# Strassen weight sums on GpSimd in operations of 256 columns, and a reordered pair of tiles

## The reference

```python
def _anemll_linear(x, w, su, sv):
    w_eff = w * (su @ sv)
    return jnp.einsum('bsh,oh->bso', x, w_eff)
a = _anemll_linear(x, gate_w, gate_su, gate_sv)
b = _anemll_linear(x, up_w, up_su, up_sv)
d = jax.nn.silu(a) * b
return _anemll_linear(d, down_w, down_su, down_sv)
...
x = x + _L0_ffn_ref(_L0_cond_ref(x, ...), ...)
x = x + _L1_ffn_ref(_L1_cond_ref(x, ...), ...)
```

## Time and profile before

| | us |
|---|---|
| median of 3 runs (lowest, highest) | 638.68 (638.6, 638.7) |
| the profiled execution's own time | 639.42 |
| its span, first to last instruction | 637.8 |
| PE busy | 627.4 |
| DVE busy | 456.0 |
| ACT busy | 319.6 |
| POOL busy | 244.9 |
| granted TensorE clock, mean | 0.998 of full speed |

### The profile page before, as it was taken

One profiled execution on the slowest core, in us unless ns is written; L12 is line 12 of the kernel. 1 busy time (PEld: TensorE's weight loads), 2 busy tenths in 40 slices (PEclk: granted clock), 3 DMA queues, 4 the chain that ended last, 5 costly groups with the idle time before them and its releaser, 6 DMA issues.

```text
span 637.8 us, 7904 instructions
## 1 busy us (share of the span) xinstructions
PE 627.4 (98%) x2864; PEld 508.0 (80%) x2864; DVE 456.0 (71%) x551; ACT 319.6 (50%) x426; POOL 244.9 (38%) x193
## 2 busy tenths in 40 slices
PE   8999999999999999999999999999999999999996
PEld 6888888888878876778777787878887888788885
DVE  4576654434467998885337888645688998999987
ACT  4685725244635344442113444425557887478860
POOL 2670020000000006752023666440003888959986
PEclk9999999999999999999999999999999999999999
DMA  8650032101021111311012000252123112222203
GB/s 249 158 162 34 26 98 74 66 1 45 20 73 47 54 34 57 142 58 59 34 33 100 33 34 30 66 107 65 56 89 100 62 59 63 99 67 67 82 0 133
DMA packets 24473, 45.18 MB, mean 71 GB/s; under 512 B 9972, under 2 KB 12020, under 8 KB 24372
## 3 DMA queue, kind: packets, MB, share of 16 engines
q1 hardware_dynamic: 21972, 40.80, 20.6%
q0 software_dynamic: 2176, 3.36, 2.0%
q10 hardware_dynamic: 288, 0.52, 0.2%
HBM read 40.74 MB, written 2.10 MB: 67 GB/s over the span
## 4 chain that ended last, share of the span: by engine, by line
PE 86%; DVE 5%; ACT 3%; issue 2%; POOL 1%; DMA 1%; DVEq 0%; SPq 0%
PE ps_down L1830 7%; PE ps_down L1831 7%; PE ps_down L1832 7%; PE ps_up L1830 4%; PE ps_up L1831 4%; PE ps_up L1832 4%; PE ps_m L2008 3%; PE ps_gate L1830 3%; PE ps_gate L1831 3%; PE ps_gate L1832 3%; PE ps_m L2009 3%; PE ps_up L2008 3%; PE ps_gate L2008 3%; PE ps_down L2008 3%; PE ps_up L2009 3%; PE ps_gate L2009 3%
## 5 line engine op out<-in xcount | busy, mean ns | idle before, releaser
L805 POOL TENSOR_TENSOR act_lo<-up,act_hi 128x512 fp32r<-128x512 f32 x14 | 18.2, 1297 | 199.0 <-ACT act_hi L1076 199.0
L1830 PE MATMUL ps_down<-act_hi,w_hi 128*128 128x512 f32 (+1 forms) x180 | 71.0, 394 | 0.0
L1831 PE MATMUL ps_down<-act_lo,w_hi 128*128 128x512 f32 (+1 forms) x180 | 70.3, 391 | 0.0
L1832 PE MATMUL ps_down<-act_hi,w_lo 128*128 128x512 f32 (+1 forms) x180 | 70.1, 389 | 0.0
L836 POOL TENSOR_TENSOR up_sum<-up_sum,up_more 128x1024 f32<-128x1024 f32 x14 | 33.8, 2411 | 66.3 <-DVE up_more L1400 66.3
L1285 DVE TENSOR_TENSOR w_lo<-w_raw,w_hi 128x512 fp32r<-128x512 f32 (+4 forms) x41 | 44.4, 1083 | 15.2 <-ACT w_hi L907 10.0
L907 ACT ACTIVATE w_hi<-w_raw 128x1024 fp32r<-128x1024 f32 (+4 forms) x30 | 27.0, 900 | 44.3 <-DVE w_raw L1292 22.3
L1830 PEld LDWEIGHTS ps_down<-act_hi,w_hi 128*128 128x128 f32 (+1 forms) x180 | 33.8, 188 | 7.4
L1832 PEld LDWEIGHTS ps_down<-act_hi,w_lo 128*128 128x128 f32 (+1 forms) x180 | 33.8, 188 | 7.2
L1831 PEld LDWEIGHTS ps_down<-act_lo,w_hi 128*128 128x128 f32 (+1 forms) x180 | 33.8, 188 | 6.7
L1400 DVE SCALAR_TENSOR_TENSOR gate_sum<-ps_up,s_group,gate_sum 128x1024 f32<-128x1024 f32 x28 | 35.8, 1280 | 4.3 <-PE ps_up L2009 4.2
(11 more groups left out here) (297 smaller groups left out, 1845.1 us busy)
## 6 DMA issues: line engine op xcount, KB each, us to landing
w_int<-in_ffn_gu SPq DMA_DIRECT2D x14, 512.0 KB, 3.5
w_raw<-in_cond_gu SPq DMA_DIRECT2D x9, 512.0 KB, 4.0
w_raw<-in_ffn_gu SPq DMA_DIRECT2D x9, 512.0 KB, 3.4
w_raw<-in_ffn_dn SPq DMA_DIRECT2D x8, 448.0 KB, 3.3
w_int<-in_ffn_dn SPq DMA_DIRECT2D x8, 448.0 KB, 3.2
xp<-in_x SPq DMA_DIRECT2D x8, 256.0 KB, 5.6
w_raw_third<-in_ffn_gu SPq DMA_DIRECT2D x4, 512.0 KB, 3.5
xp<-in_x SPq DMA_DIRECT2D x1, 2048.0 KB, 9.9
```

What stands on the lines that cost most here:

```text
L1830: nc.tensor.matmul(ps[0:m, :], w_hi[0:r, s, cols], rhs_hi(k, r), start=start and n == 0, stop=False)
L1831: nc.tensor.matmul(ps[0:m, :], w_hi[0:r, s, cols], rhs_lo(k, r), start=False, stop=False)
L1832: last = nc.tensor.matmul(ps[0:m, :], w_lo[0:r, s, cols], rhs_hi(k, r), start=False, stop=stop and n == len(ks) - 1)
```

## The change

GpSimd's block sums and low parts of 512 columns are split into two instructions of 256 columns each; the signal to the other engines stands on the second one. Ahead of a pair of tiles, GpSimd makes the next tile's sums ahead of both low parts of the former tile. ScalarE copies product 2 of a tile (tile 2's: even ahead of the Silu that ends tile 1) before it writes either high part of the former tile. VectorE scales part 0 of the next pair ahead of the former tile's two products. PE's and SP's queues are unchanged.

```diff
--- before.py
+++ after.py
@@ -792,18 +792,20 @@
                 if q == 3:
                     pool.wait_ge(w_summed, 3 * q)
                 pool.wait_ge(seven_done, 7 * (q if j == 0 else q - 1))
-                half = raw.rearrange("p (r h n) -> p r h n", r=2, h=2)
-                nc.gpsimd.tensor_tensor(low[:, pieces[1]].rearrange("p (r n) -> p r n", r=2), half[:, :, 0],
-                                        half[:, 0:1, 1].to_broadcast([P, 2, 2 * P]), ALU.add).then_inc(w_summed, 1)
+                nc.gpsimd.tensor_tensor(low[:, 4 * P:6 * P], raw[:, 0:2 * P], raw[:, 2 * P:4 * P], ALU.add)
+                nc.gpsimd.tensor_tensor(low[:, 6 * P:8 * P], raw[:, 4 * P:6 * P], raw[:, 2 * P:4 * P], ALU.add).then_inc(w_summed, 1)
                 nc.gpsimd.tensor_tensor(low[:, 12 * P:14 * P], raw[:, 4 * P:6 * P], raw[:, 6 * P:8 * P], ALU.add).then_inc(w_summed, 1)
-                nc.gpsimd.tensor_tensor(low[:, 8 * P:12 * P], raw[:, 0:4 * P], raw[:, 4 * P:8 * P], ALU.subtract).then_inc(w_summed, 1)
+                nc.gpsimd.tensor_tensor(low[:, 8 * P:10 * P], raw[:, 0:2 * P], raw[:, 4 * P:6 * P], ALU.subtract)
+                nc.gpsimd.tensor_tensor(low[:, 10 * P:12 * P], raw[:, 2 * P:4 * P], raw[:, 6 * P:8 * P], ALU.subtract).then_inc(w_summed, 1)
 
             def seven_act_lo(ph, j, c):
 
                 pool.wait_ge(act_hi_done, products_done(ph, j) + c + 1)
                 value = (up0, gate1)[c][j % 2]
-                nc.gpsimd.tensor_tensor(act_lo[:, j, chunk(c)], value[:, :], act_hi[:, j, chunk(c)].bitcast(F32),
-                                        ALU.subtract).then_inc(act_ready, 1)
+                for half in (slice(0, CT // 2), slice(CT // 2, CT)):
+                    tokens = slice(c * CT + half.start, c * CT + half.stop)
+                    last = nc.gpsimd.tensor_tensor(act_lo[:, j, tokens], value[:, half], act_hi[:, j, tokens].bitcast(F32), ALU.subtract)
+                last.then_inc(act_ready, 1)
 
             for ph in (named["ffn0 gate/up a"], named["ffn0 gate/up b"]):
                 if ph.part:
@@ -813,13 +815,13 @@
                         for c in range(CH):
                             seven_act_lo(ph, 0, c)
                         continue
-                    if j > 0:
+                    if j > 0 and not before_pair(ph, j):
                         seven_act_lo(ph, j - 1, 0)
-                        if before_pair(ph, j):
-                            seven_act_lo(ph, j - 1, 1)
                     if 1 < tile_of(ph, j + 1) and j + 1 < ACT_TILES:
                         seven_sums(ph, j + 1)
-                    if j > 0 and not before_pair(ph, j):
+                    if j > 0 and before_pair(ph, j):
+                        seven_act_lo(ph, j - 1, 0)
+                    if j > 0:
                         seven_act_lo(ph, j - 1, 1)
                 for c in range(CH):
                     seven_act_lo(ph, ACT_TILES - 1, c)
@@ -1085,6 +1087,7 @@
                     piece_hi(ph, 2, piece)
                 for c in range(CH):
                     seven_act_hi(ph, 0, c)
+                m2_to_sbuf(2)
                 act.wait_ge(gate1_done, 2)
                 nc.scalar.activation(gate1[1][:, :], gate1[1][:, :], ACT.Silu).then_inc(gate1_silu, 1)
 
@@ -1094,14 +1097,11 @@
                 if q == 1:
                     second_seven_tile(ph, bank)
                     return
-                if q == 2:
-                    m2_to_sbuf(q)
-                if j > 0:
-                    seven_act_hi(ph, j - 1, 0)
                 if q > 2:
                     m2_to_sbuf(q)
                 if j > 0:
-                    seven_act_hi(ph, j - 1, 1)
+                    for c in range(CH):
+                        seven_act_hi(ph, j - 1, c)
                 if nxt is ph:
                     piece_hi(ph, j + 1, 0)
                     if q > 0 and not before_pair(ph, j):
@@ -1573,14 +1573,13 @@
 
                 q, (bank_a, bank_b, _) = tile_of(ph, j), seven_banks[j % 2]
                 d, e = diff[j % 2], part_sum[j % 2]
+                if before_pair(ph, j) and q != 1:
+                    pair_product(ph, j + 1, 0)
                 if j > 0 and q != 1:
                     seven_products(ph, j - 1)
                 if nxt is not ph:
                     tile_product(nxt, 0, 0)
-                elif before_pair(ph, j):
-                    if q != 1:
-                        pair_product(ph, j + 1, 0)
-                elif q > 0 and j not in PAIR_FIRST:
+                elif q > 0 and j not in PAIR_FIRST and not before_pair(ph, j):
                     tile_product(ph, 0, j + 1)
                 if q > 0:
                     seven_diff(ph, j)
```

## The result

The changed kernel took 644.0 us (median of 4 runs, 642.38 to 644.56) against 638.69; the ratio is 1.0078, with a 95% interval of 1.0059 to 1.0098. Six more runs of the same kernel later gave 642.88 (642.39 to 643.96) against 638.78, ratio 1.0056 (1.0044 to 1.0068). The profiled execution took 642.38 us.

What follows compares the result with a forecast made beforehand. PE bounds the kernel, with a GpSimd-VectorE loop of 10.27 us level with its tile. Stage losses of 1.3 and 2.0 give +3.3 us: 642.7 profiled, 642.0 median, range 638.6 to 644.2.

Steps and rivals of the forecast that it cites:

- What bounds the kernel: PE, busy 627.4 of 637.8 us; its five listed waits offer some 2.9 us at most, GpSimd and VectorE blocking each other.
- Part 1, the loop: GpSimd's 256-column split, from low part over sums to next tile's low part: grows by 0.5 to 10.75 us, passing PE's tile.
- Part 2, the copy: Tile 2, ScalarE's copy of product 2 first: 1.08 us gained, then lost at products 5 and 6, net 0.
- Part 3, product 2 of tile 4: VectorE scaling first: 0.86 us gained at the scales, lost as product 2 waits for piece 1's low part, starting 0.2 later.
- T: End of VectorE's scaling for tile 4, 258.52 us before the change; forecast 0.35 us late, between 0 and 0.9.
- the race ahead of the third sum: Before tile 4's product 2: GpSimd's first half starts 0.04 us ahead of VectorE's low part, which waits for it.
- Part 4, the push: GpSimd's low parts run behind the pair's sums, so the next loop starts at T + 8.6, 1.45 us later.
- The sum: Both Strassen stages: first +1.3 us, second +2.0, together +3.3; profiled 642.7, median 642.0.
- The signs: Waits for diff or part_sum in tile 2, product 2 of tiles 4 and 11, products 5 to 7 in 4, 5, 11, 12.
- The median: Whole program: the median stood 0.74 us below the profiled execution, so profiled 642.7 becomes 642.0.
- The rival that more blockings would give 5.5 us: VectorE loses races given to it, 0.46 to 0.7 us each; loop 11.2, time 644.2 us; chance 0.16.
- The rival that the removed waits stay removed: Halves block VectorE less, loop stays below PE's 10.3 us; 0.9 to 2.9 us gained, 636 to 638; chance 0.15.

## Why the prediction was right

It had 642.0 us in 638.6 to 644.2 and slower by 3.3; measured were 644.0 and 642.88 in two sets, and 3.84 on the ruler. The first set's median is 5.3 above before and lies 0.2 under the upper end of the range, so that it fell inside is in part luck; the ruler is what bears the forecast out. By its own steps:

- *What bounds the kernel.* It says five waits of PE; the earlier trace rows has four (one, one and two). "Some 2.9 us" was the estimate for five; nothing else rests on it.
- *Part 1, the loop.* Forecast 10.75, measured 10.74 and, in the split alone, 10.76. By the sum the longer loop is worth about 0.5 in each stage, 1.0 together; undoing the split in the changed kernel gave 0.93. The half: 0.73 with a step of 0.70 taken, 0.74 and 0.70 measured. The estimate of 0.56 by the GPSIMD Engine Reference of the Trainium skill (3.1, side-by-side cycle accounting) would have made the split free; this case's rows don't agree with it, and they decided.
- *Part 2, the copy.* "I take 0": -0.33 alone. Product 5 of tile 2 was forecast at 245.87, and began at 245.16 + 0.83 = 245.99; product 6 at 247.9, and began at 248.01. But the reason, that VectorE gets there at its own pace, was only half of it. Two of VectorE's instructions ahead of `diff`, before and then after:

```profile
240.82 1.81 DVE L1285 TENSOR_TENSOR w_lo<-w_total,w_hi 128x768 fp32r<-128x768 f32 x1
...
243.94 0.69 DVE L1542 TENSOR_TENSOR up<-up,gate 128x512 f32<-128x512 f32 x1
```

```profile
240.00 1.26 DVE L1285 TENSOR_TENSOR w_lo<-w_total,w_hi 128x768 fp32r<-128x768 f32 x1
...
242.57 1.24 DVE L1542 TENSOR_TENSOR up<-up,gate 128x512 f32<-128x512 f32 x1
```

The 0.55 that the half saves in the low part is lost again in the product. The prediction had that 0.55 as its bound, with "nothing else takes its place"; something did, and that it cost the same 0.55 was luck: the prediction has no reason for it. Either engine's share can be removed by itself: without GpSimd's hold the wait of 1.09 fell to 0.25, and with `diff` first in VectorE's queue (in the sums-first kernel) it was gone.
- *Part 3, product 2 of tile 4.* T was late by 0.35: 257.36 + 0.68 = 258.04 against 258.52 - 0.83 = 257.69, so 0.35. The low part ended at T + 3.94 (260.73 + 1.25), forecast T + 3.91. Product 2 at 262.03 + 0.83 = 262.86, forecast 262.8. That GpSimd would win the race ahead of the third sum by 0.04 held: its half started at 260.68, VectorE at 260.73.
- *Part 4, the push.* Tile 3's first low part at T + 8.6 forecast, at T + 8.64 measured (266.68).
- *The sum.* First stage +1.3, measured 1.50; second +2.0, measured 2.34. Product 6 of tile 5 was forecast at 281.5 and began at 280.75 + 0.83 = 281.58. Up to product 6 of tile 5 the first stage had +1.2, measured 1.32; up to product 6 of tile 12 the second had +2.0, measured 3.71 - 1.50 = 2.21. Behind these products another 0.18 and 0.13 were lost, where the sum had 0.1 and nothing. That makes up the 0.5 that is missing. The signs named waits in tiles 4, 5, 11 and 12; the list has them in 4 and 11 only, and in 5 and 12 the lateness shows without one.
- *The median.* Added to 638.69, the ruler gives 642.5. The first set of four runs had another 1.5 us, which the step from the profiled execution to the median can't foresee; where two profiled executions differed by as much, it was in the opening, not in the change.

The rival that more blockings would give 5.5 us did not happen, although its 644.2 is near the first median. The rival that the removed waits stay removed hung on a half step of 0.62; the step was 0.70, so its condition was not met. But the half's price did not decide the matter: undivided, the same orders still cost 2.91, and with the sums first in every tile the waits stayed away at a step of 0.70. The rule that issue order decides who blocks (the Trainium skill, SBUF — State Buffer, Who interferes with whom) held in the rows shown here. That short GpSimd instructions then favour VectorE was true with the sums first, where they gained 5.4 us, and not in the change's own order, where they cost 0.93.

## What to carry to other kernels

When a chain over several engines is as long as the bottleneck's own tile, a removed wait says nothing until the next late input is found; write the chain out in rows, with each handover, and see what it becomes. Splitting instructions to let another engine in paid here only with the low parts off that chain: take them off it first (by putting the sums, which PE's next tile waits for, ahead of the low parts, which are wanted much later), then split. Compare kernels by a stretch between two rows of the same program where its opening varies, here by 1.6 us for a change of 3.84.

## What the runs showed of the hardware

- A VectorE instruction with two inputs in SBUF that starts while a GpSimd one with two is under way ends 0.55 us (512 columns) after it; a GpSimd instruction that meets such a VectorE one is 0.46 us longer (0.74 to 1.20). With an input in PSUM VectorE took 0.68 throughout. The order in which they win repeated in the two profiled executions of the changed kernel, at margins of 0.04 us. At 0.01 the starts in the trace don't tell the winner: in the undivided kernel with the sums first VectorE, at 264.40, got in ahead of GpSimd at 264.39.
- GpSimd's write of zeros, 512 columns, took 0.52 to 0.53 us in all 28 cases, two in a row started 0.46 apart where nothing held the second, and a VectorE low part of 768 columns that started under it took its free 0.95. Its subtraction of 512 columns took 1.28, of 256 columns 0.74: about 0.2 us of an instruction don't depend on its length.
- The opening of the program put the same kernel's stages at 227.64 or at 229.23 us.
